# Gathers of a two-layer transformer kernel: wait for the third one back, with a small fill between

## What is computed

```
x = layernorm(x + linear_attention(x))                   # 16 heads, elu + 1
x = layernorm(x + moe(x, experts=8, top_k=2, hidden=512, capacity=1.2 N / 8))
x = layernorm(x + causal_attention(x))                   # ALiBi, 16 heads, 4 x 1024 tokens
x = layernorm(x + moe(x, experts=32, top_k=4, hidden=128) + shared_expert(x))
```

## Time and profile before

| | us |
|---|---|
| median of 3 runs | 1375.52 |
| lowest, highest | 1374.19, 1379.01 |
| the profiled execution | 1375.22 |
| its span in the profile | 1373.5 |
| TensorE busy | 1068.0 (78%) |
| VectorE busy | 816.8 (59%) |
| ScalarE busy | 548.4 (40%) |
| GpSimd busy | 473.0 (34%) |
| of it `f_got` x128 | 127.9, 999 ns each |

### The profile page before, as it was taken

How to read it: one execution, slowest core, us unless ns; L and a number is a source line. 1 busy time by engine, 2 the same in 40 slices (tenths; PEclk the granted TensorE clock), 3 DMA queues, 4 the chain that set the end, 5 groups by cost and what they waited for, 6 DMA issues and landing times. The chain is left out here.

```text
span 1373.5 us, 20824 instructions
## 1 busy us (share of the span) xinstructions
PE 1068.0 (78%) x7039; PEld 635.6 (46%) x7039; DVE 816.8 (59%) x2124; ACT 548.4 (40%) x880; POOL 473.0 (34%) x468
## 2 busy tenths in 40 slices
PE   4762129922899999999999998988899779888851
PEld 3662117721244344534445444433488668764521
DVE  4766750032867877677877788779146424454532
ACT  1430004413056556645566654545553324321221
POOL 3110025446315210540025410424343515555654
PEclk9985559975579999979999999999999989998975
DMA  3114003422213211211113223351155566431121
GB/s 107 62 61 149 1 13 108 118 50 70 81 44 83 62 38 42 63 61 25 53 49 100 66 74 87 84 179 46 49 150 158 162 186 174 133 83 38 35 73 50
DMA packets 111908, 112.19 MB, mean 82 GB/s; under 512 B 17445, under 2 KB 95013, under 8 KB 108773
## 3 DMA queue, kind: packets, MB, share of 16 engines
q1 hardware_dynamic: 74054, 72.00, 18.5%
q0 software_dynamic: 12048, 25.71, 6.7%
q10 hardware_dynamic: 25704, 13.18, 3.3%
HBM read 65.22 MB, written 41.94 MB: 78 GB/s over the span
## 5 line engine op out<-in xcount | busy, mean ns | idle before, releaser
L2134 DVE TENSOR_REDUCE maxima<-psum 128x1 f32<-128x512 f32 (+4 forms) x624 | 390.7, 643 | 122.4 <-PE psum L1953 61.5
L2071 ACT ACTIVATE probs<-psum 128x1024 f32<-128x1024 f32 (+3 forms) x384 | 300.8, 809 | 288.4 <-PE psum L1968 215.6
L1948 PE MATMUL psum<-ka,qa 75*128 75x512 bf16 (+3 forms) x528 | 167.8, 350 | 23.5 <-DVE maxima L2134 13.8
L114 POOL DMA_INDIRECT f_got<-expert_out,dense x128 | 127.9, 999 | 129.0 <-DMA f_got<-expert_out,dense 73.9
L1981 PE MATMUL psum<-probs,v_wide 128*32 128x512 f32 (+3 forms) x1536 | 169.7, 515 | 0.0
L1441 POOL DMA_INDIRECT sorted<-x_rows,to_row x76 | 76.3, 1004 | 212.4 <-ACT probs L2071 109.5
L1964 PE MATMUL psum<-qa,ka 78*128 78x512 bf16 (+3 forms) x528 | 145.9, 339 | 3.6 <-DMA qa<-max_parts 1.5
L2468 ACT ACTIVATE g_silu<-psum 128x512 f32<-128x512 f32 x80 | 47.7, 596 | 201.0 <-PE psum L2403 83.3
L1377 POOL DMA_INDIRECT w_gu<-expert_out,to_row x64 | 64.4, 1006 | 146.2 <-ACT probs L2071 104.6
L2379 PE MATMUL psum<-w_gu,g_xT 128*128 x384 | 100.9, 408 | 14.0 <-issue 6.9
L1968 PE MATMUL psum<-mask_k,ident_b 128*128 128x128 bf16 x512 | 107.4, 228 | 0.0
(11 more groups left out here) (326 smaller groups left out, 1721.7 us busy)
## 6 DMA issues: line engine op xcount, KB each, us to landing
g_rows<-sorted SPq DMA_DIRECT2D x192, 64.0 KB
expert_out<-g_y ACTq DMA_DIRECT2D x48, 256.0 KB
qa<-q_steps SPq DMA_DIRECT2D x30, 192.0 KB
ka<-k_steps SPq DMA_DIRECT2D x10, 576.0 KB
w<-in_W SPq DMA_DIRECT2D x16, 256.0 KB
w_gu<-in_gu SPq DMA_DIRECT2D x4, 1024.0 KB
sorted<-blank SPq DMA_DIRECT2D x64, 64.0 KB
q_steps<-w_gu SPq DMA_DIRECT2D x12, 256.0 KB
```

What stands on the lines that cost most here:

```text
L114: self.pool.indirect_dma_start(oob_is_err=False, **transfer).then_inc(self.landed[u], 16)
L1948: mm = pe.matmul(bank[:, h * width:(h + 1) * width], qa[b][0:ROWS_MAX, h0 + h, qt * P:(qt + 1) * P], ka[b][0:ROWS_MAX, h0 + h, seg * HALF: ...
L2071: act.activation(probs[k % PRING][:, 2 * pair:2 * pair + 2, 0:w], PS[:, 2 * pair:2 * pair + 2, 0:w], ACT.Exp).then_inc(exps, 1)
L2134: dve.tensor_reduce(maxima[:, seg, h0:h0 + heads, qt], bank[:, 0:heads * width].rearrange("p (h k) -> p h k", h=heads), AX.X, ALU.max).the ...
```

## The change

The list of semaphores gets three entries in place of two, both for the 40 gathers of the first experts (`AHEAD`) and for the 128 of the last stage (`AHEAD_GOT`). So a gather waits for the one three back. The scatters keep two (`AHEAD1`). Both kinds of gather also get a pause: between the landing wait and the DMA GpSimd fills a small tile of its own, `between`, 128 partitions of 64 fp32 elements, that nobody reads, and waits on a new semaphore, `paused`, until this fill is complete. The first three gathers of each stage have neither wait nor fill. What is computed stays as it is.

```diff
--- before.py
+++ after.py
@@ -98,21 +98,37 @@
         engine.wait_ge(sem, count)
 
 
-AHEAD, AHEAD1 = 2, 2
+AHEAD, AHEAD1 = 3, 2
 
 
 class Spaced:
 
 
-    def __init__(self, pool, landed):
-        self.pool, self.landed, self.count = pool, landed, 0
+    def __init__(self, pool, landed, pause=None):
+        self.pool, self.landed, self.pause, self.count = pool, landed, pause, 0
 
     def start(self, **transfer):
         lap, u = divmod(self.count, len(self.landed))
         if lap:
             self.pool.wait_ge(self.landed[u], lap * 16)
+            if self.pause:
+                self.pause()
         self.pool.indirect_dma_start(oob_is_err=False, **transfer).then_inc(self.landed[u], 16)
         self.count += 1
+
+
+class Pause:
+
+
+    def __init__(self, between, paused):
+        self.between, self.paused, self.count = between, paused, 0
+
+    def __call__(self, pool):
+        def pause():
+            self.count += 1
+            pool.memset(self.between[:], 0.0).then_inc(self.paused, 1)
+            pool.wait_ge(self.paused, self.count)
+        return pause
 
 
 def wait_landed(engine, landed, count):
@@ -862,7 +878,7 @@
         with nc.Block() as block:
             @block.gpsimd
             def _(pool):
-                spaced = Spaced(pool, landed)
+                spaced = Spaced(pool, landed, G.pause(pool))
                 for e in range(E0):
                     if e >= RING:
                         pool.wait_ge(xT_psum, e - RING + 1)
@@ -2246,7 +2262,7 @@
 LEFT = K1 * TB - FINISH[LAST - 1].paced
 COUNT_AT, TABLE_AT = 8, 15
 CLEAR_FROM, CLEARS = 13, 3
-GOT_RING, AHEAD_GOT = 3, 2
+GOT_RING, AHEAD_GOT = 3, 3
 SUMS_BESIDE_GROUPS = {31: (0, 0), 35: (0, 1), 38: (1, 0), 41: (1, 1), 45: (2, 0)}
 SUMS_BESIDE_CHUNKS = {(0, 1): (2, 1), (1, 0): (3, 0), (2, 0): (3, 1), (2, 3): (4, 0),
                       (3, 3): (4, 1), (4, 3): (5, 0), (5, 3): (5, 1), (6, 3): (6, 0), (7, 3): (6, 1)}
@@ -2621,7 +2637,7 @@
 
             @block.gpsimd
             def _(pool):
-                spaced, gathers = Spaced(pool, landed), Spaced(pool, got_landed)
+                spaced, gathers = Spaced(pool, landed), Spaced(pool, got_landed, G.pause(pool))
                 for i in range(FINISH[LAST - 1].paced, K1 * TB):
                     k, t = divmod(i, TB)
                     if i == FINISH[LAST - 1].paced + 5:
@@ -2670,6 +2686,7 @@
 
         G.x_rows = M.sb("x_rows", [P, TILES, C])
         G.blank = M.sb("blank", [P, C])
+        G.pause = Pause(M.sb("between", [P, 64]), M.sem("paused"))
         G.ident, G.ones = M.sb("ident", [P, P]), M.sb("ones_sb", [P, P])
         G.ones_b, G.before_b = M.sb("ones_b", [P, P], bf16), M.sb("before_b", [P, P], bf16)
         G.lane_b, G.tile_after_b = M.sb("lane_b", [P, P], bf16), M.sb("tile_after_b", [P, TILES], bf16)
```

## The result

The changed kernel took 1400.98 us, the median of 4 runs (1400.16 to 1403.71), against 1374.86 us for the kernel before (4 runs, 1369.66 to 1379.01). The ratio is 1.0197, its 95% interval 1.0158 to 1.0237: slower by 2.0%. Forecast were 1397.5 us and a range of 1380 to 1408.

A forecast was written before the change was run, and what follows sets the result against it. The prediction took GpSimd's queue of 128 last-stage gathers, 1.82 us each on average, to set the end. Adding 20.7 us there and 1.6 in the first expert stage to 1375.22 gave 1397.5 us, range 1380 to 1408.

The forecast's parts named there:

- Step 1: Gathers of both stages: the third back started 5.97 us earlier, landing and restart took 4.66, so none waits for a landing.
- Step 2: GpSimd's queue: gather 0.99, fill with its wait 0.31, exposed preparation 0.68, so a period of 1.99 us everywhere.
- the forecast's own second way: Period by the fill's printed duration, 0.16 us, with a wait of 0.08 behind it: 1.93 us.
- Step 3: Last stage's 128 gathers: 123 intervals of 1.99 us, two with a normalisation; 256.1 us against 235.4, +20.7 us.
- Step 4: First expert stage's 40 gathers: five take 9.95 us against TensorE's 9.79, so the last turn waits for the last landing, +1.6 us.
- The sum: Whole kernel: profiled 1375.22 us plus 20.7 for the last stage and 1.6 for the first expert stage, 1397.5 us.
- The preparation runs beside the fill: Rival in GpSimd's queue between fill and gather: period 1.31 us, about 1312 us; at half effect 1.65, about 1354; chance 0.10.
- VectorE holds the fill back: Rival: GpSimd's SBUF writes meet VectorE's, 1401 us, at most 1437; held or dearer fill above 1408 has chance 0.08.
- No change: Rival: period near 1.82 us, quiet stretches lose what crowded ones win; needs preparation plus fill 0.17 us cheaper; chance 0.05.

The follow-up runs named there:

- fill_loose: The changed kernel, but GpSimd waits for the fill three back, four tiles in turn, so the wait never blocks: 1456.81 us, 1.0593 of the kernel before.
- fill_wide: The changed kernel with a fill of 128x512 instead of 128x64: 1459.25 us, 1.0610 of the kernel before.
- loose_wide: The changed kernel with a 128x512 fill before every gather and a wait for the fill before, which never blocks: 1359.48 us, 0.9865 of the kernel before.
- fill_every_second: The changed kernel with fill and wait in front of every second gather only: 1351.38 us, 0.9823 of the kernel before.
- fill_every_third: The changed kernel with fill and wait in front of every third gather only: 1342.00 us, 0.9719 of the kernel before.
- loose_mid: The changed kernel with a 128x256 fill before every gather and a wait for the fill before, which never blocks: 1343.72 us, 0.9757 of the kernel before.
- third_alone: The kernel before with waits for the third gather back and no fill: 1455.04 us, 1.0563 of the kernel before.
- five_ahead: The changed kernel with five semaphores instead of three, so waits for the fifth gather back: 1390.38 us, 1.0100 of the kernel before.

## Why the prediction was right

**Step 1, the landing wait goes.** Right: none is put down to a landing, before 58 were the earlier trace rows.

**Step 2, the period.** The mechanism was right: a wait in front of an indirect DMA exposes its preparation, here 0.77 us idle, before 0.76 behind ScalarE. `fill_loose` shows it by taking the wait's block away, 0.77 to 0.16, with the fill left in place. The size was a little off: 1.93 us in the last stage, 1.95 in the first, where 1.99 was forecast. The mis-sized term is the fill with its wait, taken as 0.31 us from start to start. These are 0.16 of fill and 0.15 of idle time before a tensor operation, while the preparation of 0.68 was worked out with only 0.08 for such a hand-over. The sum so counted 0.07 us twice. Measured are 0.17 for the fill and 0.77 behind it, which holds hand-over and preparation together. By the forecast's own second way, the printed duration with 0.08, it would have been 1.93. The Trainium skill, "Perfetto Trace Analysis", GPSIMD Engine Instruction, advises to go by the spacing of starts, and the period measured that way is the 1.93 us. But a piece of the spacing holds what the next instruction needs, and that is another one here.

**Step 3, the last stage.** Forecast 256.1 us, measured 254.74. Two errors cancel. The two intervals with a normalisation were 4.67 and 3.98, forecast 4.69 and 3.99. The other 123 took 243.4 us: at 1.935 us each they would be 238.0, 6.8 us under the forecast 244.8; the remaining 5.4 us are a few long intervals, above all 3.23 before 1249.41 and 4.71 before 1357.71. The prediction had none of these. They are the 61st and the 113th interval of the chain. The kernel before has long ones at the same two places, 2.68 and 3.24. The 113th is long in every kernel above, 3.2 us where no blocking fill stands in front of it (the kernel before and seven others) and 4.65 to 5.08 in the six where one does, however early or late it comes. So it belongs to a place in the program and not to the traffic of the moment. What it is wasn't tried. VectorE's sums don't explain it, since most gathers beside sums start 1.93 to 2.05 us apart, and neither does a fetch of instructions: in 13 of the 14 traces no packet of an instruction queue runs in this interval.

**Step 4, the first expert stage.** Forecast +1.6 us, measured 272.29 - 270.33 = 2.0. The number is near, but by luck: the mechanism was wrong for the end of the stage. The forecast let the five gathers of an expert (9.95 us) become slower than TensorE's turns and had the last turn wait for the last landing. The last five took 9.77 us, and TensorE has no idle time in front of its last turn: it is busy with the expert before from 267.66 on without a break. From the fifth turn on it never waits for rows. The time is lost at the start of the stage, where the gathers have no lead yet: TensorE stands 0.61 us before its second turn and 1.34 before the third, which comes at 223.44. In the kernel before it has no idle time there:

```profile
221.33 0.71 PE L900 MATMUL psum<-ident,rows 128*128 128x128 f32 x5
```

So the third turn is already 2.1 us late, and the later ones inherit that. In `fill_wide`, with a period of 2.31 us, TensorE does stand before every later turn, 0.96 to 2.65 us, as the forecast had it for 1.99.

**The sum.** 1375.22 + 19.3 + 2.0 = 1396.5 us; the profiled execution took 1400.16. Of the 3.7 us between, 3.5 lie in unchanged stages.

**The rivals.** "The preparation runs beside the fill" didn't occur, and its price was wrong by more than 100 us. At a period of 1.31 us it was to give 1312 us; `fill_loose` ran at 1.33 and took 1457. The chain alone was priced and no limit on the other side was looked for, other than that of TensorE's work. At 1.65 us, priced at 1354, the mechanism does what was said: `loose_wide` at 1.70 took 1359, `fill_every_second` at 1.62 1351. "VectorE holds the fill back" didn't occur: the fills are 142 to 170 ns long, with a median of 165, so none was held through a burst of sums; the 23 that run beside sums take 145 to 166 ns. "No change" needed a cheaper fill, and not even a fill of 128x1 gives it, at 1.88 us and 1.0087.

## What to carry to other kernels

A wait that never blocks is nearly free in front of an indirect DMA, and one that always blocks costs the DMA's preparation, 0.6 us here, each time: so the number of ahead, the fill and the wait for the fill are three edits with three prices, and each should be timed alone. If a pause between gathers is wanted, work that GpSimd does without being waited for gives the pause without the exposed preparation, and the best distance is to be found by a sweep. Pace the gathers against what the other engines need, since a shorter distance between them can make the kernel 80 us slower. And look for idle time in front of an instruction before a landing is taken as what it waits for.

## What was not expected of the hardware

Indirect DMAs issued 1.30 to 1.33 us apart without a break bring the other engines nearly to a stand, while the DMA engines' share of busy time falls from 0.53 to 0.25. At 1.49 us apart, or with 1.93 us at every third, nothing of it is seen. So there is a cliff between 1.33 and 1.49 us of mean distance. It is not the number in flight by itself: `fill_every_third` and `loose_mid` have the same three semaphores as `third_alone`, and `five_ahead` has more.

What exactly starves is open. VectorE could start an operation 0.03 us behind ScalarE's end in the midst of it (1156.22 + 0.60 to 1156.85), so not each hand-over is late. But instructions that wait for nothing are late too. SyncE issued 4 loads of `g_rows` from 1150 to 1200 us, where the kernel before issued 40. Its four belong to one group, and the program has only register instructions between them. SyncE's timeline of this stretch, first in the kernel before, then in `third_alone`:

```profile
1151.68 36.70 SPq L2317 DMA_DIRECT2D g_rows<-sorted  x40
```

```profile
1166.78 11.94 SPq L2317 DMA_DIRECT2D g_rows<-sorted  x4
```

The kernel before issued ten groups in 36.70 us, with the waits between them, and most groups took it 1.58 us from the first issue to the last. The one group of `third_alone` takes 11.94 us. So SyncE's issue of instructions is itself slowed. That the other engines stand because they wait for loads that come so late is likely in part, but not shown.

The Trainium skill says in "Runtime: NRT & Kernel Launch", Instruction fetch mechanics, that each sequencer fetches its next instructions in blocks by a DMA queue of its own. If those fetches queued behind the gathers' descriptors, engines would stand for long and one after another. The traces show such fetches, as packets of two instruction queues: 6 from 1150 to 1200 us in the kernel before, 2 in `third_alone`. None of them runs between 1166 and 1179 us, so no fetch that arrived ended one of SyncE's pauses there, and late fetches don't explain its slow issue. Whether they have a part in the longer stands of the other engines is open: no kernel was tried in which the others execute few instructions, or none new.
